# Cross-attention and its out-projection in one program per layer, the projection's pieces placed between the attention's steps

## What is computed

```
layer 0: 32 query heads, 8 key heads, head size 128 (q and k normalised)
layer 1: 16 query heads, 4 key heads, head size 96
kv   = concat(context, layernorm(x))            # 375 + 112 = 487 rows
out  = softmax(q k^T * scale) v                 # four query heads share a key head
x    = x + tanh(g_xattn[layer]) * (out @ Wo)    # layer 1: out @ Wo.T
x    = x + tanh(g_ffn[layer]) * ffn(layernorm(x))
```

## Time and profile before

| | |
|---|---|
| three executions | 3024.57, 3026.83, 3027.17 us |
| profiled execution | span 3023.0 us (its own time is not listed apart; the span is 3.8 us under the median) |
| PE matmul busy | 2842.8 us, 94% of the span |
| DVE, ACT, POOL busy | 1164.5, 1214.6, 710.5 us |
| attention of layer 0, from first memset to last copy | 1141.4 to 1590.2 us |
| out-projection of layer 0, to the next stage's first load | 1591.1 to 1916.5 us |
| attention of layer 1 | 2542.3 to 2771.0 us |
| out-projection of layer 1 | 2771.9 to 2954.2 us |

### The profile page before, as it was taken

The page is one execution under the profiler, slowest core; times in us unless marked ns, Lnnn a source line. Parts: engine busy times, 40 slices in busy tenths (PEclk is TensorE's granted clock), DMA queues, the critical chain, the costliest instruction groups (busy, mean ns, idle before and its releaser), DMA issues. The chain is left out here.

```text
span 3023.0 us, 43041 instructions
## 1 busy us (share of the span) xinstructions
PE 2842.8 (94%) x14487; PEld 2421.8 (80%) x14487; DVE 1164.5 (39%) x2034; ACT 1214.6 (40%) x2550; POOL 710.5 (24%) x585
## 2 busy tenths in 40 slices
PE   6999999799999997999998999598998998998997
PEld 5888887688888886888886888477998997887885
DVE  4333330411112116777772332643101112776335
ACT  4333332322222216777772323434322223785223
POOL 1111110300000005666655732120000001553400
PEclk9999999899999998999998999798998999999998
DMA  4233333222221213333336721102241222332312
GB/s 143 77 101 101 100 102 112 100 63 68 67 61 61 62 55 110 106 106 106 107 88 158 179 65 55 66 1 79 82 117 56 92 92 79 81 83 71 87 34 63
DMA packets 331149, 259.89 MB, mean 86 GB/s; under 512 B 190160, under 2 KB 285768, under 8 KB 331056
## 3 DMA queue, kind: packets, MB, share of 16 engines
q1 hardware_dynamic: 331056, 258.63, 29.3%
HBM read 190.66 MB, written 67.91 MB: 86 GB/s over the span
## 5 line engine op out<-in xcount | busy, mean ns | idle before, releaser
L42 PE MATMUL kv_y<-kv_whi,kv_xthi 128*125 128x512 f32 (+1 forms) x1152 | 446.0, 387 | 4.6 <-DVE kv_wlo L295 4.2
L44 PE MATMUL kv_y<-kv_whi,kv_xtlo 128*125 128x512 f32 (+1 forms) x1152 | 434.7, 377 | 0.0
L43 PE MATMUL kv_y<-kv_wlo,kv_xthi 128*125 128x512 f32 (+1 forms) x1152 | 433.9, 377 | 0.0
L42 PE MATMUL q_y<-q_whi,xthi 128*128 128x512 f32 (+1 forms) x1008 | 386.3, 383 | 8.0 <-ACT q_qn L487 4.7
L44 PE MATMUL q_y<-q_whi,xtlo 128*128 128x512 f32 (+1 forms) x1008 | 376.7, 374 | 0.0
L43 PE MATMUL q_y<-q_wlo,xthi 128*128 128x512 f32 (+1 forms) x1008 | 376.2, 373 | 0.0
L1000 DVE TENSOR_TENSOR at_ptlo<-at_tb,at_pthi 125x448 fp32r<-125x448 f32 (+1 forms) x384 | 238.2, 620 | 143.8 <-ACT at_pthi L953 137.9
L42 PE MATMUL o_y<-o_whi,o_ohi 128*128 128x512 f32 (+1 forms) x672 | 267.3, 398 | 14.4 <-DVE o_olo L1163 12.1
L953 ACT ACTIVATE at_pthi<-at_tb 125x448 fp32r<-125x448 f32 (+1 forms) x384 | 210.1, 547 | 136.2 <-PE at_tb L909 131.9
L43 PE MATMUL o_y<-o_wlo,o_ohi 128*128 128x512 f32 (+1 forms) x672 | 263.9, 393 | 0.0
L44 PE MATMUL o_y<-o_whi,o_olo 128*128 128x512 f32 (+1 forms) x672 | 263.8, 393 | 0.0
(11 more groups left out here) (192 smaller groups left out, 4819.9 us busy)
## 6 DMA issues: line engine op xcount, KB each, us to landing
kv_xin<-in_ctx_dram SPq DMA_DIRECT2D x48, 500.0 KB
q_raw<-in_L_xattn_Wq_dram SPq DMA_DIRECT2D x8, 2048.0 KB, 8.5
o_raw<-in_L_xattn_Wo_dram SPq DMA_DIRECT2D x64, 256.0 KB, 2.6
qT_d<-q_stage SPq DMA_DIRECT2D x56, 256.0 KB, 2.6
at_qr<-qT_d SPq DMA_DIRECT2D x64, 224.0 KB, 3.2
o_rb<-rT_d SPq DMA_DIRECT2D x32, 448.0 KB
v_d<-kv_stage SPq DMA_DIRECT2D x48, 250.0 KB
kT_d<-kv_stage SPq DMA_DIRECT2D x48, 250.0 KB, 4.5
```

Of the source, the lines that this page charges most:

```text
L42: pe.matmul(out, stat_hi, mov_hi, start=start, stop=False)
L43: pe.matmul(out, stat_hi, mov_lo, start=False, stop=False)
L44: return pe.matmul(out, stat_lo, mov_hi, start=False, stop=stop)
```

## The change

`attention` and `out_project` become one function, `attend`, with one program per layer; both loops over units are written out straight. The units are now ordered key head by key head: group g is the eight sequences of key head g. `oT` is gone: DVE's `take_o` multiplies a unit's output by the spread reciprocals (`rb`) as it leaves PSUM, ACT's and POOL's `cut_o` cut it into `oh` and `ol`. While group g+1 is attended to, the out-projection of group g is done in 14 pieces. A piece is one tile of 128 tokens times half of the output columns, summed over the group's heads only, in one PSUM bank `y`; DVE adds each piece to x (`add`). One piece stands behind T0 (`project_early`) and one behind T2 (`project_late`). The pieces of the last group stand at the end.

In layer 1 the four heads of 96 are packed into three blocks of 128 rows (`head3` spreads the fourth head's 96 rows over the three). Scores use three PSUM banks instead of four, so that `y` has one. The reciprocals go to DRAM unit by unit (`spread_sums`, 448 values, each a run of its own) and come back (`fetch_sums`). Wo comes in slabs, two ahead (`load_slab`), one in a unit: eight per group in layer 0, six in layer 1.

```diff
-      dram(f"rT{n}_d", (BATCH, L.heads, QLEN)))
+      dram(f"rT{n}_d", (L.units, G, QLEN)))
...
-        def attention(tag, L, oT, rinv):
-        def out_project(tag, L, oT, rinv, wo, x_sb, gate, source=None):
+        def attend(n, L, x_sb, wo, source=None):
...
+            D, U, NB = L.d, L.units, BATCH
+            tag = f"at{n}"
+            flip = not L.normed
+            NG = L.kvh
+            NK = G * D // P
+            NS = 2 * NK
+            PIECES = 2 * TT
+            RAW = 2
+            gate = gates[:, n:n + 1]
+            def slab_step(m):
+half, j = m // NK, m % NK
+return half * 4 + j if not flip else m if half == 0 else 4 + j
...
+            def early_of(u):
+g, k = u // NB, u % NB
+return PIECES * (g - 1) + 2 * k - 1 if g and k else None
+            def late_of(u):
+g, k = u // NB, u % NB
+return PIECES * (g - 1) + 2 * k if g and k < NB - 1 else None
...
+            def piece(q):
+g, i = q // PIECES, q % PIECES
+if g < NG - 1:
+    return g, i // TT, i % TT
+return g, i % 2, i // 2
+            def units_for(g, t):
+return g * NB + (t * P + P - 1) // QLEN + 1
...
+padded, x_loaded = sem(f"{tag}_padded"), sem(f"{tag}_xl")
+qk_loaded, v_loaded, r_loaded, r_stored = ([sem(f"{tag}_{w}{p}") for p in range(2)] for w in ("qkl", "vl", "rl", "rst"))
...
+        def load(u):
+            g, b, p = u // NB, u % NB, u % 2
+            if u >= 2:
+                sp.wait_ge(q_cut, u - 1)
+                sp.wait_ge(k_cut, u - 1)
...
+            sp.dma_start(kr[:, p, CTX:KVLEN], kl_d[g, :, b * QLEN:(b + 1) * QLEN]).then_inc(qk_loaded[p], 16)
+            if u >= 2:
+                sp.wait_ge(v_cut, u - 1)
...
+        def load_slab(w):
+            g, m = w // NS, w % NS
+            half, j, r = m // NK, m % NK, w % RAW
+            if w >= RAW:
+                sp.wait_ge(w_lo_s, w - RAW + 1)
...
+        def spread_sums(u):
+            sp.wait_ge(inverted, u + 1)
+            sp.dma_start(rT_d[u].rearrange("h s -> s h"), rinv[:, u % 2, :], allow_slow_non_contiguous=True).then_inc(r_stored[u % 2], 16)
+        def fetch_sums(u):
+            sp.wait_ge(r_stored[u % 2], 16 * (u // 2) + 16)
+            if u >= 2:
+                sp.wait_ge(o_taken if flip else o_lo, u - 1)
+            sp.dma_start(rb[:, u % 2, :, :], rT_d[u:u + 1].broadcast_to([D, G, QLEN])).then_inc(r_loaded[u % 2], 16)
...
+        for u in range(U):
+            spread_sums(u)
+            if u + 2 < U:
+                load(u + 2)
+            if u % NB in SLAB_AT and slabs < NG * NS:
+                load_slab(slabs)
+                slabs += 1
+            fetch_sums(u)
...
+        def cut_o(u):
+            g, b, p = u // NB, u % NB, u % 2
+            cols = slice(b * QLEN, (b + 1) * QLEN)
+            pool.wait_ge(o_hi, u + 1)
+            pool.tensor_tensor(ol[:, g % 2, :, cols], on[:, p, :, :], f32(oh[:, g % 2, :, cols]), ALU.subtract).then_inc(o_lo, 1)
+        def cut_slab(w):
+            i, j = w // NK, w % NK
+            pool.wait_ge(w_hi_s, w + 1)
+            pool.tensor_tensor(w_lo[:, i % 3, j, :], raw[:, w % RAW, :], f32(w_hi[:, i % 3, j, :]), ALU.subtract).then_inc(w_lo_s, 1)
...
+            if u + 2 < U:
+                cut_k(u + 2)
+                cut_q(u + 2)
+            if u >= 1:
+                cut_o(u - 1)
+            if u + 1 < U:
+                cut_v(u + 1)
+            if not flip and u % NB in SLAB_AT:
+                cut_slab(slabs_by(u))
+        cut_o(U - 1)
...
+        def project_piece(q, bank):
+            g, half, t = piece(q)
+            i = 2 * g + half
+            pe.wait_ge(w_lo_s, NK * (i + 1))
+            pe.wait_ge(o_lo, units_for(g, t))
+            for k in range(NK):
+                last = product(pe, bank[:], oh[:, g % 2, k, t * P:(t + 1) * P], ol[:, g % 2, k, t * P:(t + 1) * P],
+                               w_hi[:, i % 3, k, :], w_lo[:, i % 3, k, :], k == 0, k == NK - 1)
+            last.then_inc(projected, 1)
...
+        def turn_slab(u):
+            if flip and u % NB in SLAB_AT:
+                w = slabs_by(u)
+                done = pieces_by(u) + (early_of(u) is not None)
+                if done:
+                    pe.wait_ge(added, done)
+                if w:
+                    pe.wait_ge(w_lo_s, w)
+                pe.wait_ge(raw_loaded[w % RAW], 32 * (w // RAW) + 32)
+                for m in range(G):
+                    last = pe.transpose(y[:, m * P:(m + 1) * P], raw[:, w % RAW, m * P:(m + 1) * P], ident[:])
+                last.then_inc(w_turned, 1)
...
+                scores(u + 1, 0)
+            turn(u, 0)
+            project_early(u)
+            if more:
+                scores(u + 1, 1)
+            turn(u, 1)
+            turn_slab(u)
+            if more:
+                scores(u + 1, 2)
+            if u:
+                multiply(u - 1, 2)
+            turn(u, 2)
+            project_late(u)
+            if more:
+                scores(u + 1, 3)
+            if u:
+                multiply(u - 1, 3)
+            multiply(u, 0)
+            turn(u, 3)
+            multiply(u, 1)
+        multiply(U - 1, 2)
+        multiply(U - 1, 3)
+        first = PIECES * (NG - 1)
+        for i in range(PIECES):
+            pe.wait_ge(added, max(first, first + i - 3))
+            project_piece(first + i, tail_banks[i % 4])
...
+        def cut_o(u):
+            g, b, p = u // NB, u % NB, u % 2
+            act.wait_ge(o_taken, u + 1)
+            if g >= 2 and b == 0:
+                act.wait_ge(projected, PIECES * (g - 1))
+            act.activation(oh[:, g % 2, :, b * QLEN:(b + 1) * QLEN], on[:, p, :, :], ACT.Copy).then_inc(o_hi, 1)
...
+        for u in range(U):
+            more = u + 1 < U
+            high(u, 0)
+            if u + 2 < U:
+                cut_q(u + 2)
+            high(u, 1)
+            if more:
+                exp(u + 1, 0)
+                exp(u + 1, 1)
+            if u % NB in SLAB_AT:
+                cut_slab(slabs_by(u))
+            high(u, 2)
+            if more:
+                exp(u + 1, 2)
+            if u:
+                cut_o(u - 1)
+            high(u, 3)
+            if more:
+                exp(u + 1, 3)
+        cut_o(U - 1)
...
+        def invert(u):
+            p = u % 2
+            dve.wait_ge(exped, G * u + G)
+            if u >= 2:
+                dve.wait_ge(r_stored[p], 16 * (u // 2))
+            dve.reciprocal(rinv[:, p, :], rsum[:, p, :]).then_inc(inverted, 1)
...
+        def take_o(u):
+            p = u % 2
+            dve.wait_ge(multiplied, KVT * u + KVT)
+            dve.wait_ge(r_loaded[p], 16 * (u // 2) + 16)
+            ov = o[p][0:D, :].rearrange("d (h s) -> d h s", h=G)
+            if not flip:
+                dve.tensor_tensor(on[:, p, :, :], ov, rb[:, p, :, :], ALU.mult).then_inc(o_taken, 1)
+                return
+            if u >= 2:
+                dve.wait_ge(o_lo, u - 1)
+            for j in range(NK):
+                dve.tensor_tensor(on[D:P, p, j, :], ov[head3(j), 3, :], rb[head3(j), p, 3, :], ALU.mult)
+            dve.tensor_tensor(on[0:D, p, :, :], ov[:, 0:NK, :], rb[:, p, 0:NK, :], ALU.mult).then_inc(o_taken, 1)
...
+            more = u + 1 < U
+            invert(u)
+            if u + 2 < U:
+                cut_k(u + 2)
+            if more:
+                neg_max(u + 1, 0)
+            low(u, 0)
+            if early_of(u) is not None:
+                add(early_of(u), y)
+            if more:
+                neg_max(u + 1, 1)
+            low(u, 1)
+            if flip and u % NB in SLAB_AT:
+                cut_slab(slabs_by(u))
+            if more:
+                neg_max(u + 1, 2)
+            low(u, 2)
+            if late_of(u) is not None:
+                add(late_of(u), y)
+            if more:
+                neg_max(u + 1, 3)
+            if u:
+                take_o(u - 1)
+            low(u, 3)
+        take_o(U - 1)
+        first = PIECES * (NG - 1)
+        for i in range(PIECES):
+            add(first + i, tail_banks[i % 4])
+next_stage()
```

More of the change, by code:

```diff
@@ new lines, in _ @@
+                        sp.wait_ge(padded, 2)
+                        load(0)
+                        load(1)
+                        if source is not None:
+                            for t in range(TT):
+                                sp.dma_start(x_sb[:, t, :], source[t * P:(t + 1) * P, :]).then_inc(x_loaded, 16)
+                        slabs = 0
+                        for w in range(RAW):
+                            load_slab(w)
+                            slabs += 1
[5 more added lines that the diff above has]
+                                load_slab(slabs)
+                                slabs += 1
+                            fetch_sums(u)
@@ new lines, in _ @@
+                        cut_q(0)
+                        cut_v(0)
+                        cut_k(1)
+                        cut_q(1)
+                        for u in range(U):
[8 more added lines that the diff above has]
+                                cut_slab(slabs_by(u))
```

(44 more changed lines are left out.)

453 lines of the change are left out of this document (140 added, 313 removed).

## The result

The changed kernel takes **4351.85 us** (median of 4 runs, 4344.57 to 4359.38) against 3026.8 before: 1.438 times as long, 95% interval 1.436 to 1.440. Its profiled execution has a span of 4343.8 us, 1320.8 more than before. The forecast was slower, 3630, with a range to 3750: right in sign and, as the rows will show, in the chain of waits, but the time lies 602 us beyond the range's end.

What follows compares the result with a forecast made beforehand. PE bounded the kernel before; after the change, late key loads and POOL's slab cut would stall it. Layer 0 +497 and layer 1 +107 make +604 on 3026.8: 3630 us, range 3285 to 3750.

Steps and rivals of the forecast that it cites:

- the landing: Layer 0's key tile, last step of SP's chain: lands 2.9 us after kl's issue, within a sum of 5.7.
- At nothing: Costs set at zero: x's load in layer 0, the 448-value write's landing (some 3 us), the three score banks.
- Rival 4: Slab and fetch, 480 KB ahead of the key tile, delay its landing 1 to 2 us: 3720 or above; chance 0.08.
- The period: Layer-0 unit with both pieces: 6.5 + 5.7 + 5.65 = 17.9 us, 20.0 with the clock.
- O: Start of V3 in a unit, from which the layer-0 period is counted; key tile there at O + 12.2.
- the clock term: Layer 0, PE at half clock after idling 5 us in each unit: 2.1 us added per unit.
- Layer 1: Sum 519 us against 412, +107; unit with slab 15.8 us, key tile at E + 4.7.
- Rival 2: PE's clock stays high through the gaps: 132 us less, about 3500; chance 0.13.
- Rival 1: Only the load wait, POOL's cut_slab done before E: layer-0 period 14.0, total 3290; chance 0.12.
- Rival 3: Loads there when asked for, PE stays the bound: 68 us gained, 50 lost at T0, 3009; chance 0.08.
- E + 3.9: Latest key-tile arrival that hides behind the early piece; E is when a unit's exp(u,3) is done.
- 68 us of gain on PE: 38.1 from layer 1's fewer matmuls, 3 from fewer slabs, stage boundaries 12 + 11 and some 2 each of half clock.

Runs made afterwards that it cites:

- e3: Changed kernel with the reciprocals' write as 112 runs of 16 bytes instead of 448 of 4 (values mixed, for the time alone): 3748.2 us.
- e5: Changed kernel with each 4-byte run written to its own 64-byte block and the fetch reading a row of Wo instead (for the time alone): 3678.3 us.
- e13: e12 with VectorE's cut_k(u + 2) moved from behind invert(u) to behind low(u, 1): 3000.9 us, ratio 0.992 to the kernel before.
- e2: Changed kernel with POOL's slab cut put ahead of its cut_o and cut_v in layer 0: 3993.9 us.
- e1: Changed kernel with SP issuing the loads of unit u+2 ahead of the reciprocals' write of unit u: 3696.4 us.
- e12: e11 with the loads of q and keys issued one unit sooner (u+3 ahead of the write of u): 3008.7 us, ratio 0.994 to the kernel before.
- e11: Changed kernel with e1, e2, 16-byte runs with matching reader, last exponential ahead of ACT's copies, V and slab loads behind the fetch: 3050.5 us, ratio 1.008 to before.
- e4: Changed kernel with the edits of e1 and e2 together (loads ahead of the write, slab cut first on POOL): 3387.9 us.

## Why the prediction was wrong in time and right in the chain

- **The step that failed: "Then the landing: kl issued at 1147.83, used at 1150.77, 2.9 us."** The landing was taken from a row in which no small write stood ahead of the load. Measured behind that write: 11.9 us in the unit shown, 11.5 in the median. The forecast itself had named the write twice, as "nearest to one query load, 0.56, which also has some 500 short runs", for SyncE's 0.6 us of issue (measured 0.53, from 1712.47 to 1713.00), and under "At nothing", where its landing was covered by a unit's time. That was right for its reader (in the change SyncE waits 64.6 us in all for the write to land, 12 times) and wrong for those behind it. The nearest row was near in the number of runs, not in what they do: 448 bytes each and read there, 4 bytes each and written beside each other here. e3 and e5 take the write's shape away, and with it 604 and 674 us.
- **Rival 4** had the place right (something ahead of the key tile delays its landing) and the cause wrong: it laid 1 to 2 us on slab and fetch. e3 leaves both and the delay goes.
- **The period.** O to the end of POOL's slab cut: forecast 6.5, measured 1710.28 + 1.29 - 1705.13 = 6.4. From there to the issue of the last key load: 5.7 - 2.9 = 2.8, measured 2.7. The landing: 2.9, measured 11.9. Key tile to the next O with the clock: 5.65 + 2.1 = 7.75, measured 6.96. Sum 20.0 against 27.9: the landing is 9.0 too much, the clock term 0.8 too large the other way. Times 56 units of groups 1 to 7 that is about 445 of layer 0's missing 506 us; the rest is group 0, whose eight units take 194 us instead of 127 (its reciprocals run from 1151.25 to 1345.69; its casts come 24.8 us apart, 1212.70 and 1237.49, instead of 12.6 to 17).
- **Layer 1.** Reciprocals in a unit with a slab 24.05 us apart (3713.92 and 3737.97) instead of 15 to 16. The keys land 8.8 us after their issue, not 2.5: 6.3 of the 8.2. `take_o`'s four instructions take 0.84 + 0.50 = 1.3 us where 1.0 was taken. For the remaining 1.6 us the clock is the likely cause, expected "near 1" and measured at 0.76: with the longer landing PE idles here too, in two units that follow each other 9.34 and 8.35 us ahead of T2:

```profile
3707.27 1.18 PE L983 MATMUL at_tb<-ident,at_p 112*125 112x112 f32 x4 [9.34 <-DVE at_ptlo L1159]
3726.17 1.18 PE L983 MATMUL at_tb<-ident,at_p 112*125 112x112 f32 x4 [8.35 <-DVE at_ptlo L1159]
```

- **The clock.** Forecast between 0.7 and 0.9 in layer 0: 0.73. Rival 2 (it stays high through the gaps) is refuted; PE's busy time rose by 209 us with 203 matmul records fewer, 5% of the span. The Trainium skill, "TensorE: Matmul & The Clock Gate", Part 1, gives a ramp penalty of under 1% of a typical span; this run does not agree with it. With the gaps gone, in e13, the clock is 1.00 from 1300 to 1900 us.
- **Rival 1** (only the load wait): POOL's slab cut released SyncE 60 times with 1356 us (from 1200 us on), so both waits were there. e2 mends the second alone and gains 358 us; e1 the first alone, 655.
- **Rival 3** (faster): e12 and e13 got there, by other means. Its point, "at or before E + 3.9 it hides behind the early piece", could not be reached by SyncE's order in the change. Its size was 18 us gained (3009), the measured ones 18 and 25; that they agree is luck, for its 18 are 68 gained less 50 lost to an exponential behind two copies, and e12 and e13 have that exponential moved ahead. Of the 68 us of gain on PE, 22.7 arrived, all in layer 1. The forecast's 38.1 for fewer matmuls lies there too; layer 0 gains 1.3 us by the marks, so its 12 us of boundary were given back, in part at least in the first head group, where PE is busy 142 of 163 us.
- **What would show it**: the casts idle 5 us and more, released by the keys (yes, 15 each); L875 released by L946 (yes); L1147 20 us apart in layer 0 (no, 28) and 15 to 16 in layer 1 (no, 24); T2 released by L1159 (yes, 977 us).

## What to carry to other kernels

A transfer's landing time is not its own alone: here a key load of 2.8 us took 10.9 behind a write of 1.8 KB. When a change puts a new transfer ahead of a load on the path, price the pair, not each by its own row, and distrust above all a write of a few bytes a run, side by side. In a queue that issues for several consumers, order the steps by when their wait ends, those that wait for nothing first; each `wait` holds everything behind it, and mending one uncovers the next (slab, then V, then the fetch). The weave was to save 68 us of PE's time and gave 25 at its best, and these came only with six changes of order on four engines and a new shape for one 1.8 KB write; which of the six were needed was not taken apart.

## What the runs showed of the hardware

- 448 runs of 4 bytes to neighbouring addresses took 10.4 us to land (7.8 to 10.4 in the other orders), the same runs 64 bytes apart 3.9, the same bytes in 112 runs of 16 bytes 3.6, and 1.8 to 2.4 in e11 to e13, where V's loads no longer stand ahead of it. Why neighbours are slow no view shows. That several writes into one block wait for each other would fit all four; it was not tested alone.
- While it is outstanding, loads of 188 and 224 KB in the same queue take 10 to 11 us instead of 3, and 7.7 us when the write comes from another engine's queue. In one of e4's late units a key load issued 2.6 us before it was used 9.1 us after its issue, with a DMA share of 0.00 over the last 2 us. In the changed kernel the DMA engines' mean busy share is 0.37, less than the 0.55 of e13's first group, where the keys land in 3.1 us: here a share that looks free said nothing of a transfer's latency.
- A key cast on VectorE took 0.40 us with GpSimd idle and 1.31 us beside a subtraction of GpSimd (e12 and e13).
- Idle stretches of PE unit after unit, 13.5 us in layer 0 and 8 to 9 in layer 1, brought the mean granted clock to 0.73 and 0.76, with PE still busy 51 and 59% of the time.
